# A four-layer graph network with an expert block on one core: 23 of 49 aggregation tiles of layers 2 to 4 multiply packed blocks of gathered rows

## What is computed

```python
h = layernorm(x) @ W_in + b_in
deg = segment_sum(ones, src) + 1;  dinv = rsqrt(deg)
for l in range(4):
    msg = segment_sum((h * dinv)[dst], src) * dinv      # sum over the edges
    ctx = mean(h, axis=0) @ Wg[l] + bg[l]
    z = relu((h + msg) @ Wl[l] + bl[l] + ctx)
    h = (z - mean(z)) * rsqrt(var(z) + eps) * gamma[l] + beta[l]
x = x + h
x = x + expert_block(layernorm(x))      # two of eight experts, chosen once for all nodes
```

## Time and profile before

| what | value |
|---|---|
| median of three runs | 3345.32 us (3343.95 to 3345.57) |
| the profiled execution: its span | 3340.5 us |
| TensorE busy | 3129.2 us, 94% |
| VectorE busy | 1989.9 us, 60% |
| ScalarE, GpSimd busy | 850.9 us and 70.6 us |
| chain that ended last, TensorE's share | 80%, of which L1342 50% |
| an adjacency load of 784 KB, issue to landing | 4.3 us, median |

### The profile page before, as it was taken

One profiled execution on the slowest core, in us unless ns is written; L12 is line 12 of the kernel. 1 busy time (PEld: TensorE's weight loads), 2 busy tenths in 40 slices (PEclk: granted clock), 3 DMA queues, 4 the chain that ended last, 5 costly groups with the idle time before them and its releaser, 6 DMA issues.

```text
span 3340.5 us, 56169 instructions
## 1 busy us (share of the span) xinstructions
PE 3129.2 (94%) x17421; PEld 1810.2 (54%) x17421; DVE 1989.9 (60%) x5304; ACT 850.9 (25%) x1934; POOL 70.6 (2%) x168
## 2 busy tenths in 40 slices
PE   6888898699999999999999999999999999979998
PEld 4666676344444444444444444444444444458887
DVE  7999999755455445545554555455555555545554
ACT  3777787411111111111111111111111111123222
POOL 0000000000000000000000000000000000000100
PEclk8999999799999999999999999999999999989999
DMA  4222212412222222221222222221222222110000
GB/s 133 79 79 79 71 49 79 115 68 75 69 67 70 74 68 67 68 76 67 67 76 69 67 67 73 72 67 67 77 78 69 76 78 74 62 34 19 17 17 19
DMA packets 134136, 225.44 MB, mean 67 GB/s; under 512 B 12277, under 2 KB 106596, under 8 KB 134018
## 3 DMA queue, kind: packets, MB, share of 16 engines
q1 hardware_dynamic: 131666, 217.53, 20.2%
q0 software_dynamic: 2352, 6.40, 0.7%
HBM read 178.17 MB, written 45.74 MB: 67 GB/s over the span
## 4 chain that ended last, share of the span: by engine, by line
PE 80%; DVE 11%; issue 4%; ACT 2%; DVEq 1%; DMA 1%; SPq 0%; ACTq 0%; POOL 0%; POOLq 0%
PE bank L1342 50%; PE bank L1212 9%; PE bank L1416 5%; PE bank L1422 5%; PE bank L1300 4%; PE bank L1230 2%; PE bank L1198 2%; PE bank L1290 2%; PE bank L1228 1%; PE bank L1236 1%; DMA tab<-in_x 1%; DVE region L865 1%; DVE region L858 1%; DVE st L870 1%; DVE region L878 1%
## 5 line engine op out<-in xcount | busy, mean ns | idle before, releaser
L1342 PE MATMUL bank<-tab,region 128*128 128x512 f16 x9604 | 2143.0, 379 | 11.4 <-DMA region<-adjacency 11.2
L1342 PEld LDWEIGHTS bank<-tab,region 128*128 128x128 fp8e4 x9604 | 940.3, 98 | 1063.0 <-DVE tab L790 17.1
L1212 PE MATMUL bank<-region 128*128 128x320 bf16 x1862 | 316.4, 320 | 49.8 <-DVE region L670 48.3
L670 DVE TENSOR_SCALAR region<-iota_w,src_col,src_w 128x640 bf16<-128x640 int16 x931 | 361.0, 437 | 0.0
L865 DVE SCALAR_TENSOR_TENSOR region<-bank,c_back,bias 128x256 f32<-128x256 f32 x196 | 94.8, 483 | 405.7 <-PE bank L1300 405.7
L1029 ACT ACTIVATE tab<-region 128x640 fp8e4<-128x640 uint8 x490 | 307.2, 712 | 18.5 <-DVE region L701 18.5
L1212 PEld LDWEIGHTS bank<-region 128*128 128x128 f16 x1862 | 232.6, 144 | 124.4 <-DVE region L670 95.7
L1127 ACT ACTIVATE sd<-mv,eps_c 128x1 f32<-128x1 f32 x196 | 57.8, 295 | 820.8 <-DVE mv L872 820.8
L862 DVE TENSOR_TENSOR region<-bank,region 128x256 f16<-128x256 f32 x196 | 83.2, 425 | 297.6 <-ACT region L1125 297.6
L1125 ACT ACTIVATE region<-bank 128x256 f16<-128x256 f32 x196 | 75.3, 384 | 594.9 <-PE bank L1290 594.9
L1416 PE MATMUL bank<-tab 128*128 128x384 f32 (+1 forms) x544 | 177.2, 484 | 2.6 <-DMA b_s<-in_L_ffn_b 2.6
(11 more groups left out here) (194 smaller groups left out, 2143.9 us busy)
## 6 DMA issues: line engine op xcount, KB each, us to landing
region<-adjacency SPq DMA_DIRECT2D x196, 784.0 KB, 4.3
adjacency<-tab SPq DMA_DIRECT2D x12, 3136.0 KB, 13.9
region<-in_x POOLq DMA_DIRECT2D x48, 128.0 KB, 2.3
out<-region SPq DMA_DIRECT2D x48, 128.0 KB, 1.7
tab<-in_x SPq DMA_DIRECT2D x1, 6016.0 KB
tab<-in_L_ffn_W SPq DMA_DIRECT2D x4, 512.0 KB, 4.2
Wg_s<-in_L_gnn_Wg SPq DMA_DIRECT2D x1, 1024.0 KB
region<-in_L_gnn_Wl SPq DMA_DIRECT2D x1, 1024.0 KB, 5.6
```

Of the source, the lines that this page charges most:

```text
L670: ins = v.tensor_scalar(hot_s[:, j, :], iota_w[:], src_col[:, ds(start + j, 1)], src_w[:, ds(start + j, 1)], ALU.is_equal, ALU.mult)
L1212: ins = mm(bank[k % 2 * 2 + half][:, 0:HALF], hot_d[:, :, j], hot_s[:, j, half * HALF:(half + 1) * HALF], start=j == 0, stop=j == WIN - 1)
L1342: ins = mm(acc[a][:, :], A_s[:, a, m, :], tab[:, here + m, :], start=m == 0, stop=m == T - 1)
```

## The change

In layers 2 to 4 the tiles 2, 4, ..., 46 (`PICKED`, 23 of them) are done in another way. In the dense form all 6,272 rows of the table are multiplied, though most have no edge into the tile. Now only those rows (position p in source tile m) that have an edge into the output tile are kept. For each of 8 groups of 16 partitions there is a list of at most 272 of the 784 candidates (16 positions times 49 source tiles); the 8 lists make 17 packed blocks of 128 x 128, and the rows of the table that belong to them are gathered from a copy of the table in HBM. What has to be done for it:

- In the build, the product for each source tile has 23 more columns (`NS`), which count each row's edges into each picked tile; ScalarE takes the sign. VectorE makes numbered candidates, SyncE stores them and loads them back in groups.
- In layer 1, VectorE picks the kept rows out of 784 candidates by rounds of MAX and MATCH_REPLACE (34 rounds for each of two batches, three rounds a tile, in tiles 0 to 23). ScalarE sends the lists to HBM and back. GpSimd then gathers the adjacency's rows of 128 bytes, 17 DMAs a tile, and stores each packed tile. SyncE loads nothing of layer 2 before all is stored.
- ScalarE writes every new row of the table to HBM as well (`rows`), and takes over the loads of x in layer 4.
- GpSimd gathers the rows of 1 KB for every picked tile of layers 2 to 4, 17 DMAs in chunks of 6, 6 and 5, into four buffers (3 x 23 x 17 = 1,173 gathers).
- TensorE does 17 matmuls for a picked tile. The turn of the tile before stands after 10 of them, its product after 16; in the dense tile behind a picked one they stand after 22 and 34.
- On VectorE, the work behind the product of a dense tile that stands ahead of a picked one is put after the picked tile's sums (`late`).
- The loops over tiles are written out; some constants share memory; two constants of the expert block are loaded later.

The core of the diff:

```diff
+PICKED = list(range(2, T - 2, 2))
+GROUP = 16
+CAP = 17
+PER_STEP = 3
+CHUNK = ((0, 6), (6, 12), (12, CAP))
+SLOTS = 4
+SPARSE_T, SPARSE_MM = 10, 16
+AFTER_T, AFTER_MM = 22, 34
+def late(l, t):
+    return l > 0 and not picked(t) and picked(t + 1)
...
+                    v.tensor_tensor(hot_s[:, j0:j1, W:W + NS], pick_id[:, 0:NS].unsqueeze(1).to_broadcast([P, j1 - j0, NS]),
+                                    src_tile[:, ds(start + j0, j1 - j0)].unsqueeze(2).to_broadcast([P, j1 - j0, NS]),
+                                    ALU.is_equal)
...
+            sp.dma_start(candD.rearrange("a p m -> p a m"), cand).then_inc(cand_out, 16)
+            sp.wait_ge(cand_out, 16)
...
+                for h in range(2):
+                    sp.wait_ge(pack_out[h], 16 * ((NS + 1 - h) // 2))
+                for l in range(1, LAYERS):
+                    for t in range(T):
...
+            def fetch_pack(q):
+                if q == 0 or q == BATCH[0]:
+                    hold(pool, pick_set, 1 if q == 0 else 2)
+                if q >= 2:
+                    hold(pool, pack_out[q % 2], 16 * (q // 2))
+                for j in range(CAP):
+                    nc.gpsimd.indirect_dma_start(pack[q % 2][:, j, :], None, A_rows,
+                                                 bass.IndirectOffsetOnAxis(ap=pick_A[:, q, j:j + 1], axis=0)
+                                                 ).then_inc(pack_in[q % 2], 16)
+            for q in range(NS):
+                fetch_pack(q)
+                if q:
+                    store_pack(q - 1)
...
+            for l in range(1, LAYERS):
+                hold(pool, rows_out[l - 1], 16 * T)
+                for q in range(NS):
+                    for j0, j1 in CHUNK:
+                        if c >= SLOTS:
+                            freed(c - SLOTS)
+                        for j in range(j0, j1):
+                            nc.gpsimd.indirect_dma_start(G[c % SLOTS][:, j - j0, :], None, tab_rows[(l - 1) % 2],
+                                                         bass.IndirectOffsetOnAxis(ap=pick_tab[:, q, j:j + 1], axis=0)
+                                                         ).then_inc(g_in[c % SLOTS], 16)
...
+                for t in range(T):
+                    gathered(l, t)
+                    if l == 0:
+                        picking(t, 0)
+                    if t and late(l, t - 1):
+                        moments(l, t - 1)
+                    split(l, t)
+                    if l == 0:
+                        picking(t, 1)
+                    if t and late(l, t - 1):
+                        normal(l, t - 1)
+                    if not late(l, t):
+                        moments(l, t)
+                        normal(l, t)
...
+                    for h, (j0, j1) in enumerate(CHUNK):
+                        g_count[(c + h) % SLOTS] += j1 - j0
+                        pe.wait_ge(g_in[(c + h) % SLOTS], 16 * g_count[(c + h) % SLOTS])
```

## The result

The changed kernel takes **4072.9 us** (median of four runs, 4060.2 to 4082.0) against 3345.0 for the kernel before: 1.2175 times as long, 95% interval 1.2147 to 1.2203. 3184 was predicted, and 3400 was the upper end of the range. So the prediction was wrong, in sign and by 889 us. Of the two executions of the changed kernel on chip 8 one took 4157.0 us, over 2% more than the other (4066.8), and is compared with nothing here.

A forecast was written before the change was run, and what follows sets the result against it. VectorE was taken to bound the pairs of layers 2 to 4, gathers hidden. Terms -212 - 84 - 2 + 5 + 52 + 39 + 5 + 31 + 5 = -161 on 3340.5, plus 4.8, gave 3184 us; range 3115 to 3400.

The forecast's parts named there:

- Rival (c): GpSimd and VectorE stop each other: three VectorE operations a tile each wait half a gather, 207 us, total 3391; chance 0.08.
- The gather's price: GpSimd's time per gather, taken as 1.0 us; 17 make 17.0 us, hidden under a pair's 18.3 up to 1.08 each.
- rival (b): GpSimd's issue becomes the bound: at 1.3 us a gather 3495 us, old time crossed at 1.19; chance 0.20.
- the gathers' late start: Start of layers 3 and 4: gathers wait for tile 48's rows, about 2.5 us show, +5 us for two layers.
- The pairs: Layers 2 and 3, dense plus picked tile: 18.3 us a pair, set by VectorE, instead of 22.9; -212 us.
- Layer 4: Pairs of 21.3 us against 24.98, as stretches after the product are longer: -84 us, and -2 for three single tiles.
- Ahead of layer 2: Layer 1 packing at 19.5 us a tile: VectorE's 13.2 us tiles +39, TensorE idle +52, list round trips +5 us.
- the round of 2.0 us: One MAX and MATCH_REPLACE round on VectorE in layer 1, three a tile: 2.0 us, between 1.2 and 3.0.
- the bubble: Layer 1 packing: each tile's fetch waits for the store before it, 2.5 us on top of 17 gathers.
- The build: Before layer 1: two more VectorE comparisons per column, +31 us (15 to 41); candidates' store and reload, +5 (0 to 15).
- What would show it: List of expected signs, such as pairs of 18.3 and 21.3 us; wrong if a gather exceeds 1.19 us or VectorE's operations lengthen.

The follow-up runs named there:

- no_gathers: Changed kernel with the 1,173 row gathers of layers 2 to 4 replaced by small GpSimd fills under the same waits, layer 1's packing gathers kept: 3277.1 us.

## Why the prediction was wrong

The five layers of the account, from the first matmul of each mean to the next; the last column is the kernel without the gathers of layers 2 to 4 (chip 14):

| stage, us | before | changed | changed, chip 0 | no_gathers |
|---|---|---|---|---|
| up to layer 1 | 635.6 | 670.4 | 668.1 | 668.1 |
| layer 1 | 574.0 | 915.4 | 771.6 | 772.0 |
| layer 2 | 563.7 | 694.6 | 547.3 | 428.3 |
| layer 3 | 563.7 | 692.6 | 547.0 | 427.9 |
| layer 4 | 613.5 | 694.5 | 598.7 | 587.5 |
| rest | 390.0 | 395.1 | 395.3 | 391.6 |
| span | 3340.5 | 4062.6 | 3528.0 | 3275.4 |

**The standstill: 535 us** (4062.6 - 3528.0), of which 144 in layer 1, 147, 146 and 96 in layers 2 to 4. No term of the sum had it. Rival (c) was the only one in which GpSimd holds up another engine, and it looked at VectorE alone, through a shared port. Against it stood the 49 plain DMAs of the earlier trace rows, rightly as far as they go: plain DMAs stall nobody, on chip 8 either. The failed step is the unspoken one, that a gather beside other work acts as a plain DMA does; the trace of before has no row on it. The Trainium skill (SBUF — State Buffer, Who interferes with whom) says that TensorE and ScalarE never wait on anyone and that DMAs don't contend with compute engines. The section is on SBUF's ports, and no run shows that a port is what holds TensorE here; but whoever takes it for all kinds of waiting is told otherwise by chips 8 and 9 (166 matmuls in 450 us), and only the runs on 14, 1 and 0 agree.

**The gather's price: mis-sized, and by the prediction's own formula this alone makes the change slower.** I took 1.0 us, "near the power operation". GpSimd is busy with one for 0.946 us, but 0.30 lie between one and the next, which I did not count: 1.25 us from start to start. At this price rival (b), 0.20, comes true: GpSimd's issue is the bound. On chip 0, four gathers and the matmuls that wait for them:

```profile
1704.52 0.95 POOL L714 DMA_INDIRECT early<-rows,early  x1 [0.30 <-issue]
1705.77 0.95 POOL L714 DMA_INDIRECT early<-rows,early  x1 [0.30 <-issue]
1706.11 1.89 PE L1630 MATMUL bank<-early,region 128*128 128x512 f16 x4 [3.04 <-DMA early<-rows,early]
1707.02 0.95 POOL L714 DMA_INDIRECT early<-rows,early  x1 [0.30 <-issue]
```

A pair there lasts 21.5 us (a picked tile's successor starts at 1709.49 and 1730.96), which is 17 x 1.25 and a little. Layers 2 and 3 gain 16.5 us each, not 106. My formula of rival (b) gives 97 + 133 = 230 us above the forecast at 1.25, some 3414; 3529.7 are 116 more. Some 69 of them lie in layer 4 (below), 43 in layers 2 and 3: worked out from 547, a layer is 23 x 21.5 + 3 x 11.45 and 18 us more, where the sum had 2.5 for the gathers' late start. The trace has both parts. The first picked tile is done 28.5 us after the layer's start (1439.7 to 1468.2), 7 more than a pair. And from there to 1952.1 the other 22 take 22.0 us each, 11 more in all, because GpSimd starts one of the layer's gathers each 1.29 us in the mean (391 of them from 1442.1 to 1945.8), not each 1.25. Rival (c) without the standstill came to nothing: VectorE is busy for 285.9 us in layer 2 on chip 0 with 391 gathers beside it, against 284.8 before, with the same 737 operations.

**The pairs.** VectorE as their bound was right in kind, and no_gathers shows its size: (428.1 - 3 x 11.45) / 23 = 17.1 us, 1.2 less than the 18.3 of the sum; TensorE waits 0.86 us a pair for U there, where the sum had 2.2. Of -212 us, -271 were there to be had in layers 2 and 3 before the gathers took all but 33.

**Layer 4: mis-sized.** Predicted -86; without gathers -26, with them -15. The kernel without gathers, two turns of a pair and the matmuls between:

```profile
2620.86 0.69 PE L1554 MATMUL bank<-ident,region 128*128 128x128 f32 x2 [4.87 <-DVE region L1037]
2621.34 2.77 PE L1628 MATMUL bank<-early,region 128*128 128x512 f16 x6
...
2623.90 1.49 PE L1564 MATMUL bank<-Wx,region 128*128 128x256 f16 x6
...
2625.61 5.42 PE L1643 MATMUL bank<-tab,region 128*128 128x512 f16 x22
...
2630.86 0.38 PE L1554 MATMUL bank<-ident,region 128*128 128x128 f32 x2
...
2644.76 0.69 PE L1554 MATMUL bank<-ident,region 128*128 128x128 f32 x2 [4.87 <-DVE region L1037]
```

The pair is 23.9 us, not 21.3. TensorE waits 4.9 us for U, and comes back slower: six matmuls in 2.77 us in place of 1.46, a product in 1.49 in place of 0.82; the granted clock is 1.00 from 2610 to 2616, before the wait, and 0.50 from 2621 to 2626, behind it (that is 2.4 and 1.2 GHz); its mean over the layer is 0.86. The second turn stands behind 22 of these matmuls, so it comes 10.0 us after the first, where the sum had 7.2, and VectorE, which needs it for the split, starts that much later. I had costed a wait of TensorE as the wait alone.

**Ahead of layer 2.** MAX and MATCH_REPLACE took 0.964 and 0.954 us, and loading the values 0.09, so the round of 2.0 us was right; tiles 0 to 23 took 12.2 us, not 13.2, some 20 us better. The packing took 24.7 us a tile on chip 0 (926.34 to 951.06, from store to store), not 19.5. Of the 5.2 us more, 4.25 are 17 times the missing 0.25 us, and 1.0 is the bubble: 3.5 us, not 2.5. From a store's start to the next gather's it is 3.1 (0.58 for the store, 2.55 of waiting for its landing), and some gathers take a little more than 1.25. Over 23 tiles this is 120 us, and the first gather came at 854.5, some 14 us later than in the working. TensorE idled for 179 us in front of the adjacency, not 52; layer 1 grew by 198, not 96. The working also has a slip of its own: it ends layer 1 after 24 tiles of 13.2 us and 24 of 11.45, but there are 49, so by its own numbers TensorE would have idled for 41 us, and the forecast would have been 3173.

**The build.** 31 + 5 us were predicted up to layer 1, 32.5 to 34.8 measured in the table's runs and 37.4 at most in others: right.

**What would show it** named a gather above 1.19 us as what makes the prediction wrong, and that has come true. It didn't name what makes up three quarters of the loss, 535 of the 728 us. That a gather's price counts was seen; that gathers stop engines which don't wait for them was not.

## What to carry to other kernels

Count what an engine needs from the start of one instruction to the start of the next, not its busy time: here 1.25 against 0.95 us decided the sign by the prediction's formula, and with plain DMAs of 0.536 us in the gathers' place the changed kernel took 3285.0. A kind of instruction that the trace doesn't show can cost the other engines too; before a kernel is built on 1,500 of them, put some hundred beside the old kernel, with nothing waiting for them, and look whether it gets longer, on more than one chip. And where an engine waits for another in a round, first shorten the round: one number gave 40 us in layer 4, where the whole change, even without the standstill, lost 185.

## What was not expected of the hardware

- On chips 8 and 9 (and on the chip of the first four runs of the changed kernel) gathers by GpSimd, one behind the other, bring TensorE, VectorE and ScalarE almost to a standstill: 166 matmuls in 450 us against 2215. On chips 14, 1 and 0 kernels with such gathers lose nothing to them (3341.8 us against 3340.7 on chip 14). Why chips differ, or whether it is the moment and not the chip, is open; the kernel before runs alike on all (medians from 3340.7 to 3348.2).
- Where it occurs, TensorE first stops 13 to 19 gathers into a row of them, and the standstill lasts beyond the last: ScalarE started 27 us after the last gather's start, with the DMA engines at rest before. Five or six gathers between two pauses hardly slowed anything (10 us in two layers).
- Plain DMAs of the same size don't do it on either kind of chip (564 us for layer 2).
- A gather costs GpSimd nearly the same for 16 rows (0.84 us) as for 128 (0.946), and as much for one row 128 times (0.946) as for scattered ones. It lands some 2.9 us after its issue, a plain DMA of GpSimd 2.3.
